# Second part of a fused two-layer kernel: selective-scan tiles worked in pairs of 128x1024

## What is computed

```python
def step(h, inp):
    x_t, dt_t, B_t, C_t = inp
    A_bar = 1.0 + A[None] * dt_t[..., None]
    B_bar = B_t[:, None, :] * dt_t[..., None]
    h = A_bar * h + B_bar * x_t[..., None]
    y_t = jnp.sum(C_t[:, None, :] * h, axis=-1)
    return (h, y_t)
```

## Time and profile before

| | us |
|---|---|
| median of three runs | 5517.21 |
| the profiled execution | 5520.1 |
| its span | 5518.3 |
| PE busy (matmuls) | 4276.4 |
| DVE busy | 3917.5 |
| ACT busy | 2735.8 |
| POOL busy | 2464.7 |

### The profile page before, as it was taken

One profiled execution on the slowest core, in us unless ns is written; L12 is line 12 of the kernel. 1 busy time (PEld: TensorE's weight loads), 2 busy tenths in 40 slices (PEclk: granted clock), 3 DMA queues, 4 the chain that ended last, 5 costly groups with the idle time before them and its releaser, 6 DMA issues. The chain is left out here.

```text
span 5518.3 us, 55172 instructions
## 1 busy us (share of the span) xinstructions
PE 4276.4 (77%) x15853; PEld 2706.3 (49%) x15853; DVE 3917.5 (71%) x6879; ACT 2735.8 (50%) x5566; POOL 2464.7 (45%) x2070
## 2 busy tenths in 40 slices
PE   6887887887778877778887778788777887777833
PEld 4555555454455545445554455545445554544511
DVE  4427778585876948678684877858587694867876
ACT  3435455454545545454554645545454554545432
POOL 1224536263463625436362553626346362543633
PEclk9999999999999999999999999999999999999965
DMA  4510102010020201102020110201002020110200
GB/s 170 187 50 28 62 5 77 12 62 32 20 74 1 81 12 47 46 8 85 1 77 16 33 61 5 77 12 62 32 20 74 1 81 12 47 47 8 73 4 4
DMA packets 69381, 248.65 MB, mean 45 GB/s; under 512 B 9456, under 2 KB 9840, under 8 KB 68592
## 3 DMA queue, kind: packets, MB, share of 16 engines
q1 hardware_dynamic: 68976, 243.67, 13.0%
HBM read 212.19 MB, written 31.46 MB: 44 GB/s over the span
## 5 line engine op out<-in xcount | busy, mean ns | idle before, releaser
L1248 POOL TENSOR_TENSOR kept<-kept,hb 128x512 f32<-128x512 f32 x768 | 970.0, 1286 | 387.9 <-DVE hb L1195 387.9
L903 ACT ACTIVATE room<-ps,row_min 128x128 f32<-128x128 f32 (+3 forms) x1024 | 539.6, 527 | 1103.4 <-DVE row_min L963 1102.4
L963 DVE CUSTOM_DVE_ANT_0 ps<-ps,causal 128x128 f32<-128x128 f32 (+3 forms) x1024 | 506.0, 494 | 672.7 <-PE ps L818 670.8
L1188 DVE TENSOR_TENSOR_SCAN hb<-a_bar,ps 128x512 f32<-128x512 f32 x768 | 895.2, 1211 | 0.0
L767 POOL TENSOR_SCALAR room<-room,head_mask 128x512 f32<-128x512 f32 x208 | 344.4, 1656 | 1116.6 <-PE ps L818 1075.4
L818 PE MATMUL ps<-room 128*128 128x128 f32 (+3 forms) x2048 | 738.7, 444 | 94.7 <-ACT room L903 62.6
L1043 PE MATMUL ps<-hid_bhi,wring 128*128 128x512 f32 x1536 | 635.4, 414 | 154.6 <-issue 130.0
L840 PE MATMUL ps<-room 128*128 128x512 f32 (+3 forms) x2048 | 732.7, 444 | 0.8 <-issue 0.8
L829 PE MATMUL ps<-ident,room 128*128 128x128 f32 x2560 | 475.7, 285 | 278.1 <-ACT room L903 276.6
L1043 PE MATMUL ps<-hid_blo,wring 128*128 128x512 f32 x1536 | 625.0, 407 | 0.0
L1128 ACT ACTIVATE a_bar<-kept,a_neg 128x512 f32<-128x512 f32 x768 | 493.8, 715 | 167.3 <-PEq L740 104.8
(11 more groups left out here) (179 smaller groups left out, 7308.5 us busy)
## 6 DMA issues: line engine op xcount, KB each, us to landing
wring<-w_hi SPq DMA_DIRECT2D x352, 512.0 KB, 3.3
kept<-in_wffn SPq DMA_DIRECT2D x22, 512.0 KB, 4.2
w_hi<-wring SPq DMA_DIRECT2D x22, 512.0 KB, 2.6
w_lo<-wrest SPq DMA_DIRECT2D x22, 512.0 KB, 2.9
xn<-in_x_fm SPq DMA_DIRECT2D x17, 512.0 KB, 3.2
out_fm<-xc SPq DMA_DIRECT2D x16, 512.0 KB, 2.6
room<-in_wmod SPq DMA_DIRECT2D x2, 1536.0 KB, 7.9
win<-in_win SPq DMA_DIRECT2D x1, 1024.0 KB, 8.9
```

The source lines that it names most:

```text
L903: act.activation(probs[:, h % 2, TRI[j]:TRI[j + 1]], bank(n % 2)[:, 0:(j + 1) * P], ACT.Exp, bias=row_min[:, n:n + 1], scale=-1.0, accum_o ...
L963: dve.tensor_tensor_reduce(bank(n % 2)[:, 0:w], bank(n % 2)[:, 0:w], causal[:, T - w:T], 1.0, 3.0e38, ALU.add, ALU.min, row_min[:, n:n + 1 ...
L1188: dve.tensor_tensor_scan(hb[:, s % 8, :], a_bar[:, s % 6, :], bank(2 + m % 2), 0.0, ALU.mult, ALU.add).then_inc(scanned, 1)
L1248: pool.tensor_tensor(acc[:, m, :], acc[:, m, :], hb[:, s % 8, :], ALU.add).then_inc(acc_done, 1)
```

## The change

Only the second part is changed. Two tiles of a half become one instruction: one B multiply over 128x1024 writes PSUM banks 2 and 3 at once, one scan runs over both tiles (slots s and s+1 of `a_bar` and `hb` lie side by side), one C multiply and one addition on POOL do both. For the second tile's state to start at 0 again, the decay in its column 0 is 0: POOL writes that zero once per pass into the three odd slots of `a_bar`, and ACT's decay leaves out column 0 of odd tiles. The additions signal two tiles at a time, and all waits are for whole pairs.

```diff
--- before.py
+++ after.py
@@ -209,6 +209,7 @@
                              "dt_ready", "u_ready", "acc_init"))
         b_spread, c_spread, a_ready, b_ready, scanned, y_ready, acc_done = (
             sem(n) for n in ("b_spread", "c_spread", "a_ready", "b_ready", "scanned", "y_ready", "acc_done"))
+        first_cols = sem("first_cols")
         z_done, z_ready, gated, out_done, out_added = (sem(n) for n in ("z_done", "z_ready", "gated", "out_done", "out_added"))
         tok_done, tok_copied, quantised, back_done, back_copied, ff_done, ff_added, out_ready, rotated = (
             sem(n) for n in ("tok_done", "tok_copied", "quantised", "back_done", "back_copied", "ff_done", "ff_added", "out_ready", "rotated"))
@@ -1124,8 +1125,8 @@
                         for m in range(IM):
                             s = IM * n + m
                             if s >= IM * first + 6:
-                                act.wait_ge(scanned, s - 5)
-                            act.activation(a_bar[:, s % 6, :], dt[:, m, :], ACT.Identity, bias=1.0,
+                                act.wait_ge(scanned, 2 * (s // 2) - 4)
+                            act.activation(a_bar[:, s % 6, m % 2:T], dt[:, m, m % 2:T], ACT.Identity, bias=1.0,
                                            scale=a_neg[:, m, n:n + 1]).then_inc(a_ready, 1)
 
                     if scan:
@@ -1170,30 +1171,28 @@
                                                      ALU.add).then_inc(ffn_added, 1)
 
                     def state(n):
-                        for half in range(2):
-                            pair = (2 * half, 2 * half + 1)
+                        spread_b, spread_c = (bank(i)[:, None, :].to_broadcast([P, 2, T]) for i in range(2))
+                        for h in range(2):
+                            s = IM * n + 2 * h
                             dve.wait_ge(b_spread, n + 1)
-                            for m in pair:
-                                s = IM * n + m
-                                if s >= IM * first + 2:
-                                    dve.wait_ge(scanned, s - 1)
-                                dve.tensor_tensor(bank(2 + m % 2), u[:, m, :], bank(0), ALU.mult).then_inc(b_ready, 1)
-                            works(n, 3 * half)
-                            for m in pair:
-                                s = IM * n + m
-                                if s >= IM * first + 8:
-                                    dve.wait_ge(acc_done, s - 7)
-                                dve.wait_ge(a_ready, s + 1)
-                                dve.wait_ge(b_ready, s + 1)
-                                dve.tensor_tensor_scan(hb[:, s % 8, :], a_bar[:, s % 6, :], bank(2 + m % 2), 0.0, ALU.mult,
-                                                       ALU.add).then_inc(scanned, 1)
-                            works(n, 3 * half + 1)
+                            if s > IM * first:
+                                dve.wait_ge(scanned, s)
+                            dve.tensor_tensor(ps[:, 2:4, :], u[:, 2 * h:2 * h + 2, :], spread_b, ALU.mult).then_inc(b_ready, 2)
+                            works(n, 3 * h)
+                            if s >= IM * first + 8:
+                                dve.wait_ge(acc_done, s - 6)
+                            if s == IM * first:
+                                dve.wait_ge(first_cols, 1)
+                            dve.wait_ge(a_ready, s + 2)
+                            dve.wait_ge(b_ready, s + 2)
+                            pair = hb[:, s % 8:s % 8 + 2, :]
+                            dve.tensor_tensor_scan(pair.rearrange("p a t -> p (a t)"), a_bar[:, s % 6:s % 6 + 2, :].rearrange("p a t -> p (a t)"),
+                                                   ps[:, 2:4, :].rearrange("p a t -> p (a t)"), 0.0, ALU.mult, ALU.add).then_inc(scanned, 2)
+                            works(n, 3 * h + 1)
                             dve.wait_ge(c_spread, n + 1)
-                            for m in pair:
-                                s = IM * n + m
-                                dve.wait_ge(scanned, s + 1)
-                                dve.tensor_tensor(hb[:, s % 8, :], hb[:, s % 8, :], bank(1), ALU.mult).then_inc(y_ready, 1)
-                            works(n, 3 * half + 2)
+                            dve.wait_ge(scanned, s + 2)
+                            dve.tensor_tensor(pair, pair, spread_c, ALU.mult).then_inc(y_ready, 2)
+                            works(n, 3 * h + 2)
 
                     def works(n, i):
 
@@ -1233,6 +1232,8 @@
                         to = hid_b if HM <= n < 2 * HM else hid_a
                         pool.tensor_tensor(to[1][:, n % HM, :], full[n % 4], to[0][:, n % HM, :].bitcast(F32), ALU.subtract).then_inc(hid_split, 1)
 
+                    if scan:
+                        pool.memset(a_bar[:, :, :].rearrange("p (a b) t -> p a b t", b=2)[:, :, 1, 0:1], 0.0).then_inc(first_cols, 1)
                     if ffn:
                         for c in range(DC):
                             pool.wait_ge(h_rounded, c + 1)
@@ -1240,12 +1241,13 @@
                             pool.tensor_tensor(h_parts[1][:, c, :], h_ln[:, c, :], h_parts[0][:, c, :].bitcast(F32), ALU.subtract).then_inc(h_split, 1)
                     for n in range(first, NS):
                         if scan:
-                            for m in range(IM):
-                                s = IM * n + m
-                                pool.wait_ge(y_ready, s + 1)
+                            for h in range(2):
+                                s = IM * n + 2 * h
+                                pool.wait_ge(y_ready, s + 2)
                                 if s >= IM:
-                                    pool.wait_ge(acc_done, s - IM + 1)
-                                pool.tensor_tensor(acc[:, m, :], acc[:, m, :], hb[:, s % 8, :], ALU.add).then_inc(acc_done, 1)
+                                    pool.wait_ge(acc_done, s - 2)
+                                pair = acc[:, 2 * h:2 * h + 2, :]
+                                pool.tensor_tensor(pair, pair, hb[:, s % 8:s % 8 + 2, :], ALU.add).then_inc(acc_done, 2)
                         for j in shares(n):
                             unit(j)
```

## The result

The changed kernel takes 5625.33 us (median of 5 runs, 5623.19 to 5627.74), the kernel before 5516.57 us beside it: a ratio of 1.0196, 95% interval 1.0182 to 1.021, so it is slower, well clear of no change. The direction was forecast, the size was not: +31.8 us were worked out, +108.8 came, and the time lies above the range.

A forecast was written before the change was run, and what follows sets the result against it. DVE was taken to bound the second part: half steps +27.5 us, edges of passes with FFN +3.7, pass without FFN +0.6, sum +31.8 on the median 5517.21, thus 5549.0 us; 8-in-10 range 5512 to 5568.

The forecast's parts named there:

- What bounds: Second part of a middle pass: DVE never pauses, busy 84.00 of 84.00 us; PE has slack.
- rival 1: Dependent DVE instructions start as early as independent ones: 0.16 us less per half step, 5470 us; chance 0.11.
- Durations: DVE's paired operations over 1024 columns: B multiply 1.231 us, scan 2.277, C multiply 1.215.
- rival 3: A pair's multiply over two PSUM banks is slow: 29 us per 0.1 us more, 5578 at 0.1; chance 0.05.
- C multiply to the next B multiply, independent: On DVE, between half steps: start to start 1.130 us, was 1.178.
- hand-over: On DVE, from an operation's end to the start of the one waiting for it: 0.034 us claimed.
- half step: DVE's B multiply, scan and C multiply of two tiles: 4.706 us against 4.612, +0.094, times 293 is +27.5 us.
- upper bound: A gap of 0.07 us, or a costly second PSUM bank: about +0.17 us per half step, +50 us in all.
- The edges: Outside the regular half steps: +0.245 us per pass with FFN, +0.31 from POOL; +3.7 us in all, +0.6 without FFN.
- first parts: The passes' parts before the changed second part, with pairs of their own: untouched, no cost.
- Rival 2: Only one of two hand-overs per half step is paid: -0.03 us each, 5513 us, no change; chance 0.07.

The follow-up runs named there:

- inc1_first: Changed kernel with each pair signalling 1 instead of 2 and the wait on the direct predecessor first in the code: 5568.13 us, ratio 1.0094.
- pool_pair: Kernel before with only POOL's additions paired, one over 128x1024 released by both C multiplies: 5515.79 us, ratio 0.9999.
- banks: Changed kernel, signals of 1, next B multiply before each C multiply from state 7, B products alternating between two PSUM bank pairs, feed-forward on two banks: 5469.94 us.

## Why the prediction was right in its sign and wrong in its size

- **What bounds.** Right: DVE, in that stretch, and nothing else took over. PE's clock stayed at 1.00 in it.
- **The sums.** They hold but for one slip: rival 1's 293 times 0.16 is 47 us, not 46.
- **Durations.** Right: 1.223, 2.285 and 1.220 us against 1.231, 2.277 and 1.215. Writing a pair over two PSUM banks costs nothing extra at 1.223 us; rival 3 falls.
- **C multiply to the next B multiply, independent.** Right: 1.14 against 1.130.
The hand-over measured 0.13 us where 0.034 stood, so a half step grew by 0.302 us instead of 0.094, 88.5 us instead of 27.5. The upper bound (a gap of 0.07) was a guess around the same row and did not cover it. The rows of DVE's order ahead of the prediction already showed two and three waits on these operations, and a row of another kind was needed for them. Run inc1_first is the prediction's half step made real: 4.72 us. Its time is 5568.13 us, still 19 over the forecast, so this step was the largest that failed, not the only one.
- **The edges.** The pieces were seen nearly as worked out (+0.33 for POOL, -0.11). Run pool_pair shows that the first one alone does not lengthen the pass by a measurable amount.
- **Not forecast at all:** 1.0 us per pass in the untouched first part, 15 us in all. inc1_first shows it too (187.19 us against 185.88), pool_pair (185.78) and banks (185.69) don't. With it, 88.5 + 15.3 + 5.6 (the small pieces, 0.37 x 15) makes 109.4, against 108.8 measured. The prediction called the first parts untouched and put them at nothing. About half goes with PE's lower clock at the start of that part; the rest, and why it comes, stays open.
- **Rival 1** (no hand-over is paid) fell: the longer gaps are there. Its half step of 4.45 us was right for a different kernel, the one that puts another operation between. **Rival 2** (only one is paid) fell too: both hand-overs measure 0.13.

## What to carry to other kernels

Merging instructions on a busy engine saves one start each (0.06 us here) only if the merged ones don't now wait for their direct predecessor; look first at what each one waits for and what stands between. Where such a wait can't be avoided, put it first in the code and signal by 1, so that the operation itself carries it (0.03 against 0.13 us). Here that halved the loss and did not turn it: 51 us over the kernel before instead of 109. Where a second buffer lets another operation go between, the waits cost next to nothing and the merge pays, 48 us here.
